# One DRAM accumulator in place of two for the results of a mixture-of-experts layer, with its scatters put in series

## What is computed

```python
x = x + _layernorm(_L0_attn_ref(...))          # attention, 4 groups of 4 heads
# _L0_ffn_ref, with flat = rmsnorm(layernorm(x)), 4096 x 512:
scores = softmax(flat @ router_w.T)             # 32 experts
topk_w, topk_ids = lax.top_k(scores, 4)         # each token goes to 4 experts
topk_w = topk_w / sum(topk_w)
g, u = split(ragged_dot(xs, w1, group_sizes), 2)   # xs: tokens sorted by expert
ys = ragged_dot(silu(g) * u, w2, group_sizes)
routed = sum over a token's 4 rows of ys * topk_w
shared = silu(flat @ sg) * (flat @ su) @ sd
out = residual + routed + shared
x = x + _layernorm(out)
```

## Time and profile before

| what | value |
| --- | --- |
| median of 3 executions | 3898.41 us (3894.68 to 3900.13) |
| the profiled execution | 3902.94 us |
| its span, first to last instruction | 3901.0 us |
| mean granted TensorE clock, as a share of full speed | 0.947 |
| PE busy over the span | 3450.9 us (88%) |
| DVE busy | 2377.4 us (61%) |
| ACT busy | 1544.9 us (40%) |
| POOL busy | 1449.2 us (37%) |
| scatters in the span | 144, first issued at 3010.8 us, last at 3791.9 us |

### The profile page before, as it was taken

One profiled execution on the slowest core, in us unless ns is written; L12 is line 12 of the kernel. 1 busy time (PEld: TensorE's weight loads), 2 busy tenths in 40 slices (PEclk: granted clock), 3 DMA queues, 4 the chain that ended last, 5 costly groups with the idle time before them and its releaser, 6 DMA issues. The chain is left out here.

```text
span 3901.0 us, 71161 instructions
## 1 busy us (share of the span) xinstructions
PE 3450.9 (88%) x20374; PEld 2950.1 (76%) x20375; DVE 2377.4 (61%) x5034; ACT 1544.9 (40%) x3460; POOL 1449.2 (37%) x1569
## 2 busy tenths in 40 slices
PE   6999996899999699999959999994898999989987
PEld 5888886788888578888858888883687777777766
DVE  5666666666666666666666666667664444444448
ACT  2443443334434243543524344342122444444443
POOL 2333331233333133333303333332422555545548
PEclk9999997899999699999969999995999999999999
DMA  1100002000000200000020000015333676767768
GB/s 54 29 15 15 29 15 100 4 26 17 15 26 17 98 12 18 23 18 18 23 93 15 15 29 15 15 44 203 126 112 95 155 196 159 175 165 171 166 148 277
DMA packets 183202, 287.34 MB, mean 74 GB/s; under 512 B 16544, under 2 KB 69024, under 8 KB 182848
## 3 DMA queue, kind: packets, MB, share of 16 engines
q1 hardware_dynamic: 150432, 204.57, 16.1%
q0 software_dynamic: 32416, 78.43, 10.2%
HBM read 201.93 MB, written 81.02 MB: 73 GB/s over the span
## 5 line engine op out<-in xcount | busy, mean ns | idle before, releaser
L424 DVE TENSOR_TENSOR ptl<-TP,pth 128x512 fp32r<-128x512 f32 (+1 forms) x640 | 407.9, 637 | 281.2 <-ACT pth L560 270.2
L282 POOL TENSOR_SCALAR oTh<-onorm 128x256 fp32r<-128x256 f32 x256 | 104.3, 407 | 1000.3 <-DVE onorm L430 1000.3
L560 ACT CAST pth<-TP 128x512 fp32r<-128x512 f32 (+1 forms) x640 | 349.5, 546 | 300.9 <-PE TP L696 297.1
L613 PE MATMUL O<-pth,vh 128*128 128x256 f32 (+1 forms) x1280 | 399.9, 312 | 22.7 <-DVE ptl L424 22.7
L274 POOL TENSOR_TENSOR work<-work,cst 128x320 f32<-128x320 f32 x128 | 132.9, 1038 | 735.2 <-ACT work L544 735.2
L412 DVE TENSOR_REDUCE negmax<-S 128x1 f32<-128x384 f32 (+7 forms) x512 | 382.3, 749 | 15.9 <-PE S L681 11.1
L613 PE MATMUL S<-wph,xTh 128*128 128x512 f32 (+1 forms) x1024 | 354.6, 346 | 7.0 <-DVE xTl L369 6.7
L615 PE MATMUL O<-pth,vl 128*128 128x256 f32 (+1 forms) x1280 | 359.4, 281 | 0.0
L614 PE MATMUL O<-ptl,vh 128*128 128x256 f32 (+1 forms) x1280 | 358.4, 280 | 0.0
L614 PE MATMUL S<-wpl,xTh 128*128 128x512 f32 (+1 forms) x1024 | 347.2, 339 | 0.0
L615 PE MATMUL S<-wph,xTl 128*128 128x512 f32 (+1 forms) x1024 | 345.7, 338 | 0.0
(11 more groups left out here) (279 smaller groups left out, 9323.1 us busy)
## 6 DMA issues: line engine op xcount, KB each, us to landing
raww<-in_L_ffn_w_dram SPq DMA_DIRECT2D x33, 1024.0 KB, 7.3
prob<-in_L_attn_x_dram SPq DMA_DIRECT2D x9, 2048.0 KB, 9.4
stage<-in_L_attn_w_aq_dram SPq DMA_DIRECT2D x68, 256.0 KB, 2.8
raww<-in_L_ffn_w_dram SPq DMA_DIRECT2D x33, 512.0 KB, 8.2
stage<-in_L_attn_w_ao_dram SPq DMA_DIRECT2D x64, 256.0 KB, 2.6
a<-acc_d SPq DMA_DIRECT2D x64, 256.0 KB, 4.1
acc_d<-x SPq DMA_DIRECT2D x1, 8448.0 KB, 31.5
x_d<-racc SPq DMA_DIRECT2D x4, 2048.0 KB, 14.2
```

The costliest lines, as they stand in the source:

```text
L282: nc.gpsimd.tensor_scalar(slot(oTh, u), onorm[:], 1.0, 1.0, ALU.mult, ALU.mult).then_inc(o_hi, 1)
L424: nc.vector.tensor_tensor(ptl[:, n % 2, 0:w], TP[:, n % 2, 0:w], pth[:, n % 2, 0:w].bitcast(F32), ALU.subtract).then_inc(tp_lo, 1)
L560: nc.scalar.copy(pth[:, n % 2, 0:w], TP[:, n % 2, 0:w]).then_inc(tp_hi, 1)
L613: mm(out, ah, bh, start=first, stop=False)
```

## The change

There is one accumulator `acc_d`. The DMA that filled the second with zeros is gone. All scatters add to the one accumulator, and the scatter of tile t now waits for that of tile t-1: in the loop `buffer_free(s, j * 16)` becomes `buffer_free(1 - s, (j + s) * 16)`, and one such wait is put ahead of the scatter of tile 1. The wait stands at the same place of POOL's queue, behind the gather and ahead of the wait for `y_ready`. The last stage loads one tile in place of two, POOL's addition is gone, and DVE waits for the load directly.

```diff
-            sp.dma_start(acc_d[1].rearrange("(t p) m -> p t m", p=P),
-                         blank[:, 0:M].rearrange("p (o m) -> p o m", o=1).to_broadcast([P, NTILE + 1, M])).then_inc(blanked, 16)
...
-                nc.gpsimd.indirect_dma_start(acc_d[s], bass.IndirectOffsetOnAxis(ap=idy[:, s:s + 1], axis=0), yb[:, s], None,
+                nc.gpsimd.indirect_dma_start(acc_d, bass.IndirectOffsetOnAxis(ap=idy[:, s:s + 1], axis=0), yb[:, s], None,
                                              compute_op=ALU.add).then_inc(y_out[s], 16)
...
             for s in range(2):
                 pool.wait_ge(hl_done, s + 3)
                 gather_rows(nc, xg, s, h_d, idx, x_in)
+                if s == 1:
+                    buffer_free(0, 16)
                 scatter(s, s + 2)
...
                     wait_apart(pool, hl_done, t + 3)
                     gather_rows(nc, xg, s, h_d, idx, x_in)
-                    buffer_free(s, j * 16)
+                    buffer_free(1 - s, (j + s) * 16)
                     scatter(s, t + 2)
             for s in range(2):
-                buffer_free(s, before * 16)
+                buffer_free(1 - s, (before + s) * 16)
                 scatter(s, pairs * 2 + s)
...
-                for dst, src in ((a0, acc_t[0]), (a1, acc_t[1])):
-                    sp.dma_start(dst[:, s], src[i]).then_inc(a_in[s], 16)
+                sp.dma_start(a0[:, s], acc_t[i]).then_inc(a_in[s], 16)
...
             for n in range(NTILE):
-                s = n % NL
-                pool.wait_ge(a_in[s], 32 * (n // NL + 1))
-                nc.gpsimd.tensor_tensor(a0[:, s], a0[:, s], a1[:, s], ALU.add).then_inc(sum_ready, 1)
-                if n >= 1:
-                    root(n - 1)
-            root(NTILE - 1)
+                root(n)
...
-                v.wait_ge(sum_ready, n + 1)
+                v.wait_ge(a_in[s], 16 * (n // NL + 1))
```

More of the change, by code:

```diff
@@ L892, in route @@
         x2_t = x2_d.rearrange("b (t p) m -> (b t) p m", p=P)
-        acc_t = acc_d[0].rearrange("(t p) m -> t p m", p=P)
+        acc_t = acc_d.rearrange("(t p) m -> t p m", p=P)
         rawf = raww[:].rearrange("p s c -> p (s c)").rearrange("p (w c m) -> p w c m", w=3, c=MC)
@@ L945, in _ @@
             store(NTILE - 1)
-            sp.wait_ge(blanked, 48)
+            sp.wait_ge(blanked, 32)
             sp.wait_ge(dense_out, 16)
@@ L1002, in _ @@
                     first_weights()
-            pool.wait_ge(blanked, 48)
+            pool.wait_ge(blanked, 32)
             pool.wait_ge(dense_out, 16)
@@ L1656, in finish @@
         sl, ac = sb("sl4", [P, FS]), sb("ac4", [P, FS])
-        a0, a1 = (sb(n, [P, NL, M]) for n in ("a04", "a14"))
+        a0 = sb("a04", [P, NL, M])
         ob = sb("ob4", [P, 2, M])
@@ L1669, in finish @@
         scattered = sem("scattered")
-        sum_ready, sh_ready = sem("sum_ready4"), sem("sh_ready4")
+        sh_ready = sem("sh_ready4")
         st, var_ready, rstd_ready, shift_ready, nrm_ready = (sem(n) for n in ("st4", "var_ready4", "rstd_ready4", "shift_ready4", "nrm_ready4"))
@@ L1683, in finish @@
         out_t = out.rearrange("b (t p) m -> (b t) p m", p=P)
-        acc_t = [acc_d[s].rearrange("(t p) m -> t p m", p=P) for s in range(2)]
+        acc_t = acc_d.rearrange("(t p) m -> t p m", p=P)
         @block.sync
@@ L1887, in build @@
     h_d = nc.dram_tensor("h_d", (NTOK + P, HW), F32).ap()
-    acc_d = [nc.dram_tensor(f"acc_d{s}", (NTOK + P, M), F32).ap() for s in range(2)]
+    acc_d = nc.dram_tensor("acc_d", (NTOK + P, M), F32).ap()
     with ExitStack() as logits:
```

## The result

The changed kernel takes 4058.43 us (median of 4, 4050.82 to 4064.38) against 3896.55 us for the kernel before (median of 4). The ratio is 1.0417, with a 95% interval of 1.0393 to 1.0440: 4% slower. The profiled execution took 4050.82 us, with a span of 4049.0 us, 148 us longer than before. The forecast was 4057 us.

A forecast was written before the change was run, and what follows sets the result against it. PE bounds the 805 us expert stage before, a scatter chain after: 841 + 108 = 949 us against 781, +168; less 8 and 1, +159 on 3902.9 gives 4062, at the median 4057 us; range 3995 to 4105.

The forecast's parts named there:

- The bound: Expert stage: each scatter awaits the previous landing, so scatters form a chain of period 5.88 us against PE's 4.83 us.
- Its first term: Expert stage: 143 scatter periods of 5.88 us (landing 4.88, way to next issue 1.0), 841 us.
- The second term: Expert stage: 31 weight loads each hold one scatter for 3.5 us more, 108 us.
- That it reaches PE: Expert stage: late gathers and late `y_free` hold PE, which runs at POOL's pace once POOL lags a few us.
- the signs: Expert stage: scatters about 5.9 us apart, previous scatter's DMA releasing well over 100 waits, first to last some 950 us.
- Last stage: Last stage: POOL's additions go and PE waits less for DVE's products; 8 us saved, bounds 2 and 13.
- The zero fill: Routing: the 8,448 KB DMA goes; 1 us saved, bounds 0 and 8.
- A: Rival, expert stage: landing comes before 3.83 us, PE keeps the pace and only the gains remain; 3889 us; chance 0.04.
- B: Rival, expert stage: only 81 quiet tiles pay, 1.05 us each, +85; 3974 us in all; chance 0.08.
- C: Rival, expert stage: granted clock falls to the 1.2 GHz level and PE binds again; about 4400 us; chance 0.03.

The follow-up runs named there:

- the wait alone: The kernel before, keeping both accumulators, where the scatter of tile t waits for that of tile t-1; 4060.91 us, ratio 1.0423.
- small loads: The changed kernel, each of the expert stage's 31 weight loads bringing 512 KB in place of 1,536 KB; 3959.55 us, ratio 1.0161.
- `y_ready` first: The changed kernel, where POOL waits for `y_ready` ahead of the previous scatter's landing and increments `y_free` behind the scatter's issue; 4040.5 us, ratio 1.0367.

## Why the prediction was right

*The bound.* The claim was that the wait for tile t-1 makes scatters a chain with the period landing plus way to the next issue, slower than PE. The runs show it from four sides: the wait alone gives the loss; a shorter way gives back about the amount worked out (18 us for 21); with half the rows, and so a shorter landing, nearly all of it comes back; less PE work gives almost nothing.

*Its first term.* Forecast 143 x 5.88 = 841 us. The landing of 4.88 us, read from two waits at L1417, came out as 4.9. One reading of the earlier trace rows was off, without effect: the DMA engines are not idle for 2.1 us behind the scatter, but from 0.9 to 2.1 us. The way was taken as 1.0 us and is 0.8 to 0.9. The period is then 5.8 us, as the median distance of 5.81 says too, and the term 829 us: the forecast had 12 us too much.

*The second term.* Forecast 31 x 3.5 = 108 us; what is left of 941 beside 829 is 112, and small loads take 90 of these away. The 30 distances above 8 us are 3.6 us above the median each, 109 us together, and the forecast had 3.5 us. The reading that in series a load holds one scatter is borne out by the timeline at 3674.53. Together 941 against 949.

*That it reaches PE.* Right, by the gather: 143 us of PE's waits. The other way that was named, `y_free`, held ACT for 143 us, but no wait of PE is put down to it, and PE's wait at `down` stayed (16.3 us for 17.9). Of the signs, the release of POOL's scatter by the DMA of the one before is not seen in the changed kernel, whose profile says "issue" 132 times; it is seen with `y_ready` first, 134 times.

*Last stage.* Forecast -8, measured -7.8. The forecast drew it from two waits of PE, 7.5 and 4.4 us; 6.4 us of them went, nearly all from the first. And the reason for the lower end of the bounds was wrong: DVE did not keep its 80.8 us, as the next section but one tells.

*The zero fill.* Forecast -1, measured -3.4 on the two profiled executions, and 3 on the mean of all profiles. Moved later it costs the same.

*The rivals.* A (hidden) is what happens at a landing of 3.7 us, but not here. B (only quiet tiles pay, 3974 us) fell: loaded tiles pay too, with 30 distances above 8 us where there were 8; and it assumed two long periods at each of 31 loads, 62 in all, while in the kernel before 49 of 143 are above 5.3 us and only 8 above 8 us. C (the clock): the granted clock of the stage fell from 0.97 to 0.92, so PE did see the 1.2 GHz level more often, but with a third of its work gone only 8 us of the stage came back. The price of C was worked out from 4.5 us of PE's work a tile; by the rows it is 5 us (716.9 us busy from first to last scatter, 143 tiles), so C would have come out higher.

That the total is only 1.4 us off is luck in part. Inside the stage 12 us too much in the first term stood against 4 too little in the second. On the profiled execution the forecast was 4062 us against 4051: 8 us too much in the stage, and some 3 us too little gain in routing and attention. The step to the median went the other way, -4.5 us in the forecast and +7.6 us as measured.

## What to carry to other kernels

When a wait on a DMA's landing is drawn from two steps back to one, compare the landing plus the way to the next issue with the period of the engine that sets the pace. Here 5.8 us stood against 4.8, and the pace went over to the DMA, with no slack for any transfer that comes between; at 4.6 the same wait was nearly free. If such a chain is needed, put every other wait ahead of the one that comes last, and split large loads that share the DMA engines, which also helped the kernel without the chain.

## What the runs showed of the hardware

In these runs, an accumulating scatter of 128 rows of 2 KB from POOL lands 4.9 us after its issue, of which POOL works 1.6 us; with 64 rows it is 3.7 us. The Trainium skill's page DMA: Bandwidth & Descriptors, section Anatomy of one DMA, would give an estimate of 2.6 us for the former; the measurement decides.

DVE's addition of two tiles in SBUF was slowed by POOL's additions beside it. The residual addition before, and in the changed kernel, with POOL's additions gone:

```profile
L1775 DVE TENSOR_TENSOR ob<-a,x 128x512 f32<-128x512 f32 x27 | 27.0, 1001 | 0.0
...
L1769 DVE TENSOR_TENSOR ob<-a,x 128x512 f32<-128x512 f32 x27 | 18.7, 692 | 0.0
```

In the experiment on the last stage alone, without POOL's additions, it took 692 ns as well, and in that on the wait alone, where POOL still adds, 1000 ns. DVE's addition with one operand in PSUM, `a<-a,O`, did not change: 677 ns before, 682 after. DVE's busy time in the last stage fell with the additions from 80.8 to 70.9 us. The Trainium skill's GPSIMD Engine Reference, section Key points, says that the two engines share SBUF interfaces and contend when DVE reads two SBUF inputs; the trace agrees.
